# Second attention of a two-layer network, computed with transposed scores

## The reference

```python
xf = jnp.transpose(x.reshape(B, C, N), (0, 2, 1))
qkv = (xf @ W_qkv + b_qkv).reshape(B, N, N_HEADS, 3 * D_K)
q, k, v = jnp.split(qkv, 3, axis=-1)
attn = jnp.einsum('bihd,bjhd->bijh', q, k) * SCALE
attn = jax.nn.softmax(attn, axis=2)            # over the keys j
res = jnp.einsum('bijh,bjhd->bihd', attn, v).reshape(B, N, N_HEADS * D_K)
res = res @ W_out + b_out + xf
```

## Time and profile before

| | |
|---|---|
| median of three runs | 1404.52 us |
| execution that was profiled | 1401.21 us |
| its span, first to last instruction | 1399.0 us |
| TensorE busy | 1302.2 us |
| ScalarE busy | 967.6 us |
| VectorE busy | 921.5 us |
| GpSimd busy | 748.9 us |
| mean granted clock of TensorE | 0.974 of 2.4 GHz |
| moved by DMA | 53.27 MB |

### The profile page before, as it was taken

How to read it: one execution, slowest core, us unless ns; L and a number is a source line. 1 busy time by engine, 2 the same in 40 slices (tenths; PEclk the granted TensorE clock), 3 DMA queues, 4 the chain that set the end, 5 groups by cost and what they waited for, 6 DMA issues and landing times.

```text
span 1399.0 us, 29958 instructions
## 1 busy us (share of the span) xinstructions
PE 1302.2 (93%) x11666; PEld 616.0 (44%) x11666; DVE 921.5 (66%) x1270; ACT 967.6 (69%) x1263; POOL 748.9 (54%) x681
## 2 busy tenths in 40 slices
PE   3169999999999999999999998799997999999998
PEld 2132222222222222222222226444454888888885
DVE  6876666666666666666666657410037999999995
ACT  3377777777777777777777773332204999999994
POOL 4166666666666666666666652200000767777772
PEclk9579999999999999999999999999999999999999
DMA  2141110111011101110111000000007222212211
GB/s 69 54 134 31 31 32 2 31 31 32 2 31 32 29 4 32 31 26 7 31 32 23 9 1 1 1 0 0 0 29 272 62 60 60 54 45 52 60 30 60
DMA packets 19922, 53.27 MB, mean 38 GB/s; under 512 B 4642, under 2 KB 7330, under 8 KB 19668
## 3 DMA queue, kind: packets, MB, share of 16 engines
q1 hardware_dynamic: 19824, 51.92, 14.1%
q10 hardware_dynamic: 4, 0.01, 0.0%
HBM read 40.95 MB, written 10.95 MB: 37 GB/s over the span
## 4 chain that ended last, share of the span: by engine, by line
PE 80%; DVE 11%; issue 3%; ACT 2%; POOL 2%; DMA 1%; SPq 1%; DVEq 0%; ACTq 0%; POOLq 0%
PE ps L898 31%; PE ps L907 17%; PE ps L889 5%; DVE aneg L773 5%; PE ps L1055 4%; PE ps L1063 4%; PE ps L1004 4%; PE ps L1014 4%; PE ps L1047 3%; DVE conv L620 2%; PE ps L1038 1%; DVE big L776 1%; POOL big L355 1%; PE ps L1026 1%; PE ps L991 1%
## 5 line engine op out<-in xcount | busy, mean ns | idle before, releaser
L898 PE MATMUL ps<-big,w 64*64 64x512 f32 x4096 | 483.5, 589 | 0.0
L479 ACT ACTIVATE big<-ps 128x1024 f32<-128x1024 f32 x256 | 262.0, 1023 | 179.0 <-PE ps L898 179.0
L674 DVE TENSOR_SCALAR big<-big 128x1024 f32<-128x1024 f32 x256 | 177.8, 694 | 263.8 <-POOL big L370 263.8
L668 DVE TENSOR_TENSOR big<-qpad,ps 128x1024 f32<-128x1024 f32 x256 | 311.0, 1215 | 7.8 <-ACT ps L458 5.4
L370 POOL TENSOR_TENSOR big<-qpad 128x1024 f32<-128x1024 f32 x128 | 244.5, 1910 | 133.2 <-PE ps L898 68.6
L370 POOL TENSOR_TENSOR big<-qpad,V 128x1024 f32<-128x1024 f32 x128 | 244.5, 1910 | 129.7 <-PE ps L898 73.5
L479 ACT ACTIVATE big<-ps,vec 128x1024 f32<-128x1024 f32 x256 | 284.0, 1109 | 0.0
L390 POOL TENSOR_TENSOR big<-BT,big 128x512 f16<-128x512 f32 x129 | 150.4, 1166 | 248.0 <-DVE big L776 248.0
L907 PE MATMUL ps<-big,w3s 128*32 128x512 f32 x2048 | 246.2, 598 | 1.3 <-ACT big L479 1.3
L898 PEld LDWEIGHTS ps<-big,w 64*64 64x64 f32 x4096 | 146.6, 133 | 205.9 <-issue 112.6
L773 DVE TENSOR_REDUCE aneg<-ps 128x1 f32<-128x1024 f32 x131 | 158.3, 1209 | 6.0 <-PE ps L1047 5.7
(11 more groups left out here) (140 smaller groups left out, 1116.5 us busy)
## 6 DMA issues: line engine op xcount, KB each, us to landing
raw<-s_f SPq DMA_DIRECT2D x32, 512.0 KB, 6.1
h1h<-q_d SPq DMA_DIRECT2D x64, 128.0 KB, 3.0
h1l<-k_d SPq DMA_DIRECT2D x64, 128.0 KB, 3.1
q_d<-XN SPq DMA_DIRECT2D x8, 512.0 KB, 2.6
k_d<-XN SPq DMA_DIRECT2D x8, 512.0 KB, 2.6
X<-in_x SPq DMA_DIRECT2D x2, 1024.0 KB, 6.3
out<-X SPq DMA_DIRECT2D x8, 256.0 KB, 2.0
m<-grid_d SPq DMA_DIRECT2D x1, 1024.0 KB, 4.6
```

Of the source, the lines that this page charges most:

```text
L479: act.activation(h2[m % H2RING], z2[m % ZRING], ACT.Relu, bias=v("cb2") if m % 2 else 0.0).then_inc(h2_ready, 1)
L668: dve.tensor_tensor(h1[m % HRING].rearrange("p (y a b) -> p y a b", y=2, b=W), u.unsqueeze(2).to_broadcast(shape), b[:, :, HALF // W * hf: ...
L674: dve.tensor_scalar(h1[m % HRING], h1[m % HRING], 0.0, None, ALU.max).then_inc(h1_ready, 1)
L898: last = pe.matmul(z2[m % ZRING][CH * y:CH * (y + 1), HALF * x:HALF * (x + 1)], w2[CH * x:CH * (x + 1), :], h1[m % HRING][CH * x:CH * (x + ...
```

## The change

Everything stands in the second attention. What it does:

- q and k rows are stacked in three groups, [high, high, low] and [high, low, high]: 96 rows (the product of the two low parts is left out). Three buffers hold three heads; a head is loaded in 6 DMAs instead of 8. The buffers of parts on their way out are four instead of two.
- Each head's scores are made twice. `along(x)` makes 128 queries x 1024 keys as before, from which VectorE takes only the negated maxima, 8 columns a head. `turn(n)` transposes these [128, 8] into [8, 128] in one instruction; ScalarE and VectorE split them in high and low (`max_high`, `max_low`), and SP moves them to two rows under the head's q rows (`move_max`), against two rows of ones under the k rows. `across(s)` then makes 128 keys x 1024 queries from 98 rows, with the maximum already subtracted, and ScalarE takes the exponent without a bias. No turning and no splitting of it is left.
- `weigh(s)` multiplies in f32, the values (128 keys x 32) being the weights, in four quarters of 256 queries on four column tiles. GpSimd adds the exponents of two steps, and `sums(j)` multiplies that with ones, on the same tiles. VectorE inverts the sums in four pieces of 64 columns (`invert`, in four different steps) and multiplies (`divide`). SP places each quarter in rT by DMA (`place_head`), so the turning of the results falls away.
- `along` runs 14 steps ahead of `across`; its first 14 blocks lie between the 16 blocks of values, which come after the projections now. Both kinds of scores and the turned maxima take the three bank pairs 0 to 5 in turn; banks 6 and 7 hold the results.
- The bias of the values is multiplied with the output weights once (`bo`) and added at the end; the values are copied by ScalarE without it. The loops are written out instead of Fori. `conv`, `gel`, `qw` and `kw` move into other buffers, for which SP waits for `k_ready` before the late weights.

The core of the diff (on SP, ScalarE, GpSimd, VectorE and TensorE):

```diff
+Q_STACK, K_STACK = [0, 0, 1], [0, 1, 0]
+ROWS = D * len(Q_STACK)
+HEADS3, PRING, AHEAD_MAX = 3, 6, 14
+TURN_LAG, PARTS = 2, 4
+QUARTER = N // 4
+SLOTS = G * NK
...
+        TURN = NK + TURN_LAG
+        def turning(x):
+            return TURN <= x < TURN + SLOTS and (x - TURN) % NK == 0
+        def turned(x):
+            return min(max((x - TURN) // NK + 1, 0), G)
...
+            for n in range(G):
+                move_max(n)
+                if n >= 2:
+                    place_head(n - 2)
+                if HEADS3 <= n + 2 < G:
+                    sp.wait_ge(st_ready, NK * (n + 2 - HEADS3 + 1))
+                    load_head(n + 2)
...
+            def load_head(n):
+                i = n % HEADS3
+                for r in range(len(Q_STACK)):
+                    sp.dma_start(QS[i][D * r:D * (r + 1), :].bitcast(fp32), q_d[Q_STACK[r], D * n:D * (n + 1), :]).then_inc(st_in[i], 16)
+                    sp.dma_start(KS[i][D * r:D * (r + 1), :].bitcast(fp32), k_d[K_STACK[r], D * n:D * (n + 1), :]).then_inc(st_in[i], 16)
+            def move_max(n):
+                sp.wait_ge(m_lo, n + 1)
+                for a in range(2):
+                    sp.dma_start(QS[n % HEADS3][ROWS + a:ROWS + a + 1, :].rearrange("o (t q) -> o t q", q=P).bitcast(fp32),
+                                 mparts[:, a, :].bitcast(fp32)).then_inc(m_in, 16)
+            def place_head(n):
+                sp.wait_ge(o_done, n + 1)
+                row, t = D * (n % HP), n // HP
+                for c in range(4):
+                    sp.dma_start(rT[row:row + D, t, QUARTER * c:QUARTER * (c + 1)], OT[n % 2][D * c:D * (c + 1), :]).then_inc(rT_in[n % 2], 16)
...
+            for j in range(SLOTS // 2):
+                pool.wait_ge(pr_ready, 2 * j + 2)
+                if j >= 2:
+                    pool.wait_ge(sums_done, j - 1)
+                pool.tensor_tensor(PSUMS[j % 2], PT[2 * j % PRING], PT[(2 * j + 1) % PRING], ALU.add).then_inc(added, 1)
...
+            for s in range(SLOTS):
+                if turning(s + AHEAD_MAX):
+                    max_high(turned(s + AHEAD_MAX) - 1)
+                act.wait_ge(st_ready, s + 1)
+                if s >= PRING:
+                    act.wait_ge(pv_done, s - PRING + 1)
+                    act.wait_ge(added, (s - PRING) // 2 + 1)
+                act.activation(PT[s % PRING], bank(2 * across_pair(s), 2), ACT.Exp).then_inc(pr_ready, 1)
...
+            for x in range(SLOTS + AHEAD_MAX + NK + TURN_LAG):
+                if turning(x):
+                    max_low(turned(x) - 1)
+                if x < SLOTS:
+                    maxes(x)
+                n, c = (x - AHEAD_MAX - NK - 4) // NK, (x - AHEAD_MAX - NK - 4) % NK
+                if 0 <= n < G and c < 4:
+                    invert(n, c)
+                elif 0 <= n < G and c == 4:
+                    divide(n)
...
+            def along(x):
+                n, it = x // NK, x % NK
+                if it == 0:
+                    pe.wait_ge(st_in[n % HEADS3], 96 * (n // HEADS3 + 1))
...
+                for hf in range(2):
+                    last = pe.matmul(bank(2 * along_pair(x) + hf), QS[n % HEADS3][0:ROWS, P * it:P * (it + 1)],
+                                     KS[n % HEADS3][0:ROWS, HALF * hf:HALF * (hf + 1)], start=True, stop=True)
...
+            def across(s):
+                n, kt = s // NK, s % NK
+                if kt == 0:
+                    pe.wait_ge(m_in, 32 * (n + 1))
+                x = s + AHEAD_MAX
+                if turning(x):
+                    pe.wait_ge(pr_ready, s)
+                elif x <= SLOTS:
+                    pe.wait_ge(mx_ready, x - (s == 0))
...
+                for hf in range(2):
+                    last = pe.matmul(bank(2 * across_pair(s) + hf), KS[n % HEADS3][0:ROWS + 2, P * kt:P * (kt + 1)],
+                                     QS[n % HEADS3][0:ROWS + 2, HALF * hf:HALF * (hf + 1)], start=True, stop=True)
+                last.then_inc(st_ready, 1)
+            def weigh(s):
...
+                pe.wait_ge(pr_ready, s + 1)
+                for c in range(4):
+                    last = pe.matmul(bank(6 + n % 2)[D * c:D * (c + 1), 0:QUARTER], V[:, n, kt, :],
+                                     PT[s % PRING][:, QUARTER * c:QUARTER * (c + 1)],
+                                     start=(kt == 0), stop=(kt == NK - 1), skip_group_check=True)
...
+            for n in range(2 * NK):
+                value(n)
+                x = n - 2
+                if turning(x):
+                    turn(0)
+                if x >= 0:
+                    along(x)
...
+            for s in range(SLOTS + 4):
+                x = s + AHEAD_MAX
+                if turning(x):
+                    turn(turned(x) - 1)
+                if x < SLOTS:
+                    along(x)
+                if s < SLOTS:
+                    across(s)
+                if 0 <= s - 2 < SLOTS:
+                    weigh(s - 2)
+                if s % 2 == 1 and s >= 5:
+                    sums((s - 5) // 2)
```

More of the change, by code:

```diff
@@ L197, in build @@
[L197 to L201, removed]
+        rT_in = [sem(f"rT_in{i}") for i in range(2)]
+        st_in = [sem(f"st_in{i}") for i in range(HEADS3)]
+        added, sums_done = sem("added"), sem("sums_done")
@@ L214, in build @@
[L214 to L219, removed]
+        qk3 = sb("qk3", [P, 2, N], fp32r)
+        part = [[x[:, 2 * i + a, :].bitcast(fp32r) for a in range(2)] for x in (XN, big[:, 4:8, :]) for i in range(2)]
@@ L307, in _ @@
+            for n in range(3):
                 send_parts(n)
             for i in range(2):
[L309 to L320 removed]
@@ L324, in _ @@
+            place_head(G - 2)
+            place_head(G - 1)
             for n in range(T):
@@ L572, in _ @@
-            for n in range(2 * T):
-                act.wait_ge(rT_ready, n + 1)
-                act.activation(rT[:, n // 2, HALF * (n % 2):HALF * (n % 2 + 1)], bank(n % 4), ACT.Identity).then_inc(rT_saved, 1)
+                if n >= PARTS:
+                    act.wait_ge(f_lo, n - PARTS + 1)
+                    act.wait_ge(parts_out[n % PARTS], 32 * (n // PARTS))
+                act.activation(part[n % PARTS][0], bank(2 * (n % 2), 2), ACT.Identity, bias=v(("bq", "bk")[which], t % CT)).then_inc(f_hi, 1)
@@ L1040, in _ @@
                 last.then_inc(p_ready, 1)
-            def scores(u):
-                i, it = u // NK % 2, u % NK
-                for jh in range(2):
-                    last = pe.matmul(bank(2 * (u % 2) + jh), QS[i][:, P * it:P * (it + 1)], KS[i][:, HALF * jh:HALF * (jh + 1)],
-                                     start=True, stop=True)
-                last.then_inc(sc_ready, 1)
-            def turn(u, hf):
-                for i in range(4):
-                    jt = 4 * hf + i
-                    last = pe.transpose(bank(4 + hf)[:, P * i:P * (i + 1)], PR[u % 2][:, P * jt:P * (jt + 1)], ident[:, :])
-                last.then_inc(pT_ready, 1)
@@ L1058, in weigh @@
-            def weigh(u, k):
-                order = list(range(4, NK)) + list(range(4))
-                for jt in order:
-                    for pT in (PTH, PTL):
-                        last = pe.matmul(bank(6 + u % 2)[:, 0:VW], pT[u % 2][:, P * jt:P * (jt + 1)],
-                                         V3[:, 2 * k + u // NK, jt, :],
-                                         start=(jt == order[0] and pT is PTH), stop=(jt == order[-1] and pT is PTL))
-                last.then_inc(oo_ready, 1)
@@ new lines, in sums @@
+            def sums(j):
+                n = j // (NK // 2)
+                pe.wait_ge(added, j + 1)
+                for c in range(4):
+                    last = pe.matmul(bank(6 + n % 2)[D * c:D * (c + 1), QUARTER:2 * QUARTER], ones[:, :],
+                                     PSUMS[j % 2][:, QUARTER * c:QUARTER * (c + 1)],
+                                     start=False, stop=(j % (NK // 2) == NK // 2 - 1), skip_group_check=True)
+                last.then_inc(sums_done, 1)
+            pe.wait_ge(f_lo, 2 * T)
```

333 lines of the change are left out of this document (128 added, 205 removed).

## The result

The changed kernel takes 1464.05 us (median of four runs, 1460.08 to 1464.77) against 1404.68 for the kernel before on the same chip: 1.041 times as long, with a 95% interval of 1.038 to 1.045, or 59 us more. The forecast was 1433, 29 more. The time lies inside the wide range, 1380 to 1505, and 9 us above the range given for the forecast itself, 1410 to 1455. The execution profiled took 1464.22, its span is 1462.4 us, and the mean granted clock fell from 0.974 to 0.932.

What follows compares the result with a forecast made beforehand. Before, TensorE, ScalarE and VectorE were nearly full together in the second attention. Gains of 4.2 us a head on work against losses of 8.7 on the wait made 29 us more than 1404.5, so 1433, range 1380 to 1505.

Steps and rivals of the forecast that it cites:

- Rival 1: Second attention: loads don't hold TensorE as read; 88 us less, 1345, or 1328 with no wait at all; chance 0.18.
- a held head: Second attention, heads whose `along` waits for late-loaded rows: 23.0 us each, twelve of them, against 18.5 a head before.
- The work, 14.3: One head of the second attention without any other wait: eight TensorE steps of 1.74 us plus 0.4.
- The term 1.08: TensorE's two score products in a step, `along` and `across`, taken as 0.54 us each.
- The added 0.4 for turning: Once a head, turning the maxima: 0.12 us on TensorE and about 0.3 of waiting for a bank pair.
- The wait, 6.3: TensorE before step 8n+2, held by a load issued behind placing: ready at 3.5, rows landed at 9.8 us.
- The clock, 2.4: After each held wait TensorE's clock falls; half of 4.9 us is lost, 2.4 us a head, bounds 0 and 3.2.
- the steps without `along`, 1.20: Fourteen steps near the second attention's end: 0.54 + 0.44 + 0.22 = 1.20 us each on TensorE.
- What was costed at nothing: Before 1027 us: reused buffers and one more wait of SP, expected to add no time.
- Rival 2: Second attention: waits come but the clock stays or returns at once; 1404 us, no change; chance 0.13.
- Rival 3: TensorE's step is cheaper, as with score products at 0.43 us a pair; VectorE bounds at 1.55; 1414 us; chance 0.09.
- Rival 4: Column-tiled products cost double, so TensorE's step is 2.39 us; 1501 us; chance 0.08.

Runs made afterwards that it cites:

- the first experiment: Changed kernel with SP loading the next head before placing the finished one, nothing else: 1355.73 us, 0.965 of the kernel before.
- the fourth experiment: Changed kernel with a fourth buffer for heads' rows and SP loading a head further ahead, before placing: 1343.82 us, 0.957 of the kernel before.
- experiment 2: Changed kernel with seven unread TensorE products ahead of the wait for the rows of heads 4 to 15: 1429.13 us, 1.018 of the kernel before.
- experiment 7: Kernel before with only SP's added wait for `k_ready` ahead of the late weights: 1404.28 us, 1.000 of before.
- experiments 9 and 10: The changed kernel and the kernel before, each run once more unchanged for the first layer's length: 1462.24 and 1406.91 us.
- experiment 8: Four-buffer, early-loading version of the changed kernel (1343.82 us) with each `along`'s two products issued twice in a row: 1401.94 us, 0.997 of the kernel before.
- experiments 5 and 6: Four-buffer, early-loading version (1343.82 us) with two weighings together every second step, ahead of `across` or behind it: 1360.62 and 1358.68 us.

## Why the prediction was right or wrong

**Direction, mechanism and place were right; the loss was half of the measured one.** Forecast were 29 us, measured 59. SP's queue, the wait for the division, the landing, the dip of the clock after each wait, twelve heads with it and a small wait at head 1 (1.4 forecast, 1.0 measured) stand in the trace as written, and the first experiment shows that this order is the cause. Rival 1 put the waits and dips together at 88 us, and 108 were measured.

**The sizes were too small, all in the held heads and what follows them.** By parts, in us, from the second attention's first product in each profile:

| part | forecast | measured |
|---|---|---|
| to the start of step 0 | 54.2 | 54.1 |
| then to the end of head 1's wait | 19.2 | 19.0 |
| then to the first held wait's end | 20.6 | 22.2 |
| eleven heads | 253.0 | 276.9 |
| from the last held wait's end to the end | 53.9 | 58.6 |
| sum | 400.9 | 430.8 |

(The forecast's numbers are its own terms, cut at the waits: 14.3 + 3.5 + 1.4 = 19.2, 14.3 + 6.3 = 20.6, 11 × 23.0 = 253.0.) The step that failed is the sum of a held head, 14.3 + 6.3 + 2.4 = 23.0. Term by term it is 25.2:

- **The work, 14.3, measured 15.3** (the fourth experiment). The term 1.08 for the two score products held by accident: they are 0.66 + 0.47 = 1.13, but made of 0.47 each, less than my 0.54, and 0.19 for the change of tiles. `weigh` is 0.57 where I took 0.44, and only `sums`, 0.43 behind column-tiled work, was right at 0.22 a step. In all 1.92 instead of 1.74. I had read the column-tiled price in the earlier trace rows, where groups of four follow each other, and had not asked what the first group behind full-array products costs. The added 0.4 for turning was not there: `turn` takes 0.2, and `along` behind it is cheaper by 0.19.
- **The wait, 6.3, measured 6.5 to 6.8.** Two errors, of which the second takes back part: the four placing issues are 0.63 apart, not 0.463 (that pitch was read from loads alone), so the last load goes out 7.25 us after `along` started instead of 6.7, and lands at 10.4, not 9.8; and TensorE stands ready at 3.8, not 3.5.
- **The clock, 2.4, measured 2.9 to 3.1** (the second and the first experiment; what is left of 25.2 after 15.3 and 6.6 is 3.3). The time to its return was mis-sized: I took 4.9 us, the shorter of the two returns in the trace of before, and it is 6.9 in the mean, near the other one, which followed an idle time like these. That one I had read as 6.3; the row's 0.77 puts the return at about 1080.5, so 6.6. Half of the time, the other part of the term, is a little too much: half of 6.9 would be 3.4, and from head to head a microsecond of return costs some 0.4. Both experiments stay under my bound of 3.2. The Trainium skill (TensorE: Matmul & The Clock Gate, HAM oscillation — how this bites in real kernels) describes a loop that pays the return at every pass; the trace agrees, in all twelve held heads.
- **Behind the held heads, the steps without `along`, 1.20, are 0.66 + 0.57 + 0.22 = 1.45**, for the same reason as the first: now `across` stands behind the column-tiled products. Fourteen of them make 3.4 of the 4.7 us by which the last part is longer.

**What was costed at nothing held.** SP's wait for `k_ready` costs nothing (experiment 7), and the first layer's later end is scatter between executions (experiments 9 and 10). The other engines' terms were near: VectorE's head is 8 × 1.22 + 4 × 0.54 + 0.42 + 0.28 = 12.6 (forecast 12.4). The Trainium skill (VectorE: DVE Perf Modes, First, the fixed hardware budget) led to the estimate of 0.76 us a reciprocal; the rows have 0.54, and the measurement decides.

**The rivals.** Rival 1 is what experiments 1 and 4 build: the same arithmetic without the wait is 4% faster than the kernel before. Rival 2 falls with experiment 2, where the clock alone is worth 35 us. Rival 3 was half right in its premise (0.47 a pair) and wrong in its result, because the changes of tiles cost more than that gains. Rival 4 falls: 1.92, not 2.39.

**What stays open.** How the 0.19 and 0.14 us of a change between tile forms arise isn't settled: experiment 8 ties the 0.19 to the place, not to a mechanism. Nor is it shown why the clock falls early in one wait and late in the next. An order that saves them and still covers the maximum and the exponent wasn't tried beyond experiments 5 and 6. Why the first layer's clock changes level at different moments wasn't tried either.

## What to carry to other kernels

Before adding a wait to a DMA queue, list what is issued behind it and when its readers come: here two blocks of a loop in the other order are worth 108 us, and a spare buffer without the new order nothing. Price a wait of several microseconds on TensorE as the wait plus the clock's return, here 6.5 + 3. Read the price of an instruction from a row where it stands behind the same neighbour as in the new order, and for the length of a stage compare two executions before explaining a few microseconds.

## What the runs showed that I had not expected

- A score product of two times 512 columns takes 0.47 us behind full-array work and 0.66 behind column-tiled products; four column-tiled products of 256 columns take 0.43 behind others of their form and 0.57 behind full-array ones.
- In waits of 6.5 to 6.8 us the granted clock stayed at 2.4 GHz for the first 1.9 to 5.0 us, and came back 5.5 to 8.8 us after work resumed, though TensorE was busy without a gap for all of them; in the trace of before it was 5.0 and 6.6. The length of a head went with it, from 24.5 to 25.9 us.
- SP's issue of a 32 KB placing takes 0.58 us and the next follows after 0.63; that of a 128 KB load follows after 0.46. The placings land in 1.8 us, the loads in 2.9 to 3.1 in the median. The Trainium skill's page on DMA: Bandwidth & Descriptors (Anatomy of one DMA — SWDGE path) gives a fit for DMAs that GpSimd issues, by which 128 KB would take 2.3, an estimate; these loads are SP's, and the rows here stay above it.
- Useless work of 6.3 us in each of twelve waits made the kernel 35 us faster.
